# Moving the rates' exponentials to GpSimd, the first state squares to ScalarE, and the fourth token group to the end of the first step

## The chip, the cores and the metric

The kernel runs as one program on one core of a Trainium2 chip. The metric is the device time of one execution in microseconds. The core's engines work from queues of their own and wait for each other by semaphores: TensorE (PE in the profile; PEld is its weight loads), VectorE (DVE), ScalarE (ACT), GpSimd (POOL) and SyncE (SP), which issues the DMAs.

## What is computed

A small two-layer network. Layer 0 is a block with a test-time-trained linear memory and a feed-forward part; layer 1 has attention and experts. The change touches only the memory of layer 0. Cut to what matters:

```python
h = _layernorm(x, axis=-1) * (1 + ca) + sa            # 4 x 512 tokens of 256
qkv = silu(h @ W_qkv); q, k = q / norm(q), k / norm(k)
lr = jax.nn.softplus(h @ W_lr + b_lr + BASE_LR_INV)   # 6 rates a token
w0n = norm(w0); w1n = norm(w1); w2n = norm(w2)        # of the first state
def step(w0, w1, w2, chunk):                          # 8 chunks of 64 tokens
    gate = k @ w0; hb = k @ w2; hidden = silu(gate) * hb
    ...                                               # gradients dhbm, dgba
    w1 += newtonschulz5(einsum(hidden * lr1, v))
    w0 += newtonschulz5(einsum(k * lr0, dgba))
    w2 += newtonschulz5(einsum(k * lr2, dhbm))
    w0, w1, w2 = (w / norm(w) * its first norm for each)
    return w0, w1, w2, silu(q @ w0) * (q @ w2) @ w1
```

The softplus of z is computed as max(z, 0) + log(1 + e), with e = exp(min(-z, z)), and the logarithm as a polynomial in e / (e + 2).

## The kernel before

Sixteen tiles of 128 tokens (a tile holds a chunk of 64 tokens of two sequences) are normed in four groups g = 0 to 3 of four tiles (`StartNorm`). For each group VectorE takes the sums, GpSimd the root of the variance (a power of -1/2 over four columns), an engine normalises the tiles (`normalize`, 256 columns each), TensorE turns the two halves of the result (`turn`, kt = 0 and 1), ScalarE scales and shifts the first half (`modulate`) and VectorE the second (`modulate_half`), into `hT`. Group 0 and 1 hold chunks 0 to 3, groups 2 and 3 chunks 4 to 7.

The rates (`LearningRates`) come in two parts: part 0 is the first four tiles (24 columns), made in the prologue, part 1 the other twelve (72 columns). For each part: TensorE projects, VectorE forms z and u = min(-z, z) (`start`), ScalarE takes v = exp(u) (`exponential`), VectorE u = 1 / (v + 2) (`ratio`), and then the polynomial follows (`finish`), on VectorE for part 0 and on GpSimd, in step 1, for part 1. Each result is told by the semaphore `step`, counted up to OPS = 14 a part.

The recurrence is written out as one `step(t)` for each engine: step 0 (`first`), a hardware loop, and the last two steps written apart. On each engine instructions run strictly in the order written. Inside a step two tables of tuples set the order: `INNER` that of TensorE's products (A, AA, Y, A1, AA1, YT, X2 are phases of the Newton-Schulz iteration, each over six matrices) with other work put between them, and `TAKEN` that of ScalarE's copies out of the PSUM banks. The entries START 0 to 6 exist in step 0 alone: 0 turns modulation rows, 1 and 2 turn group 2, 3 and 4 turn group 3, 5 projects the other rates (`project_rest`, 12 products), 6 turns their result. START 1, 3 and 5 in `TAKEN` are ScalarE's modulations and its copy of the rates. PROJECT_V is the value projection of the chunk after next (two parts before the state's update, two behind it); its first part waits for `h_copied`, GpSimd's copy of that chunk's rows of `hT` (`copy_h`). TURN_QK turns q and k of the next chunk and waits for GpSimd's scaling of them (`scale_qk`).

GpSimd's order in a step is: `hidden`, in step 1 the polynomial of the rates, in step 0 group 2's root and tiles, then `scale_qk`, `apply_rates` (products of k and v with the rates), `copy_h`. Behind steps 0 and 1 stand five operations on modulation rows (`guard_gates`).

The end of a step on VectorE: six updates of the state, sums of squares of three matrices (ScalarE squares others), `factors`, and the scaling. The norms of the first state (`start_sums`, six sums of 128 columns; `start_norms`) are made in step 0. A second set of modulation rows (`make_rows(1)`) is made by TensorE at the end of step 0, copied by ScalarE (`take_rows(1)`), and before both stands a wait for the first operation of the rates' part 1. ScalarE loads a table when a function of another set follows (`load_table`).

## Time and profile before

| | us |
|---|---|
| three runs, median | 1005.22 |
| lowest and highest of them | 1001.09, 1006.02 |
| the profiled execution, its own time | 1001.45 |
| its span, first to last instruction | 999.6 |
| busy in the span: TensorE, VectorE | 958.0, 690.0 |
| busy in the span: ScalarE, GpSimd | 573.2, 465.4 |

Times in the trace count from the span's start. The prologue of the memory lasts to about 24 us, step 0 to about 75, step 1 to about 113, and a later step takes about 38 us. An engine's row shows start and length; a bracket behind it gives the engine's idle time before and what ended it. Two rows of an engine overlap a little, since the next instruction starts while the last drains. L numbers are lines of the kernel before; a helper's line serves many places.

### The profile page before, as it was taken

The page shows a single profiled execution, that of the slowest core. Times are in us where ns is not written, and L with a number is a line of the kernel's source. Part 1 is how long each engine was busy: PE and PEld are TensorE (multiplying, and loading weights), DVE is VectorE, ACT ScalarE, POOL GpSimd, SP SyncE. Part 2 cuts the span into 40 slices and gives each one's busy share as a digit, 9 for nine tenths or more (in the row PEclk, how much of TensorE's full clock was granted, in tenths as well). Part 3 has the DMA queues.
Part 4 walks back from the last instruction along what each step waited for, and adds up shares of the span by engine and source line. Part 5 has one row for each costly group of instructions (what it writes and reads, how often), then busy time and mean ns, then how long its engine had stood idle before and what let it go on. Part 6 is the DMA issues. An engine that isn't in the chain of part 4 may idle for free.

```text
span 999.6 us, 24780 instructions
## 1 busy us (share of the span) xinstructions
PE 958.0 (96%) x9554; PEld 722.3 (72%) x9554; DVE 690.0 (69%) x2061; ACT 573.2 (57%) x1534; POOL 465.4 (47%) x425
## 2 busy tenths in 40 slices
PE   9799999999999999999999899999999999999987
PEld 7668788788787656574647678786878696868646
DVE  5998898998999822314132776867686668676874
ACT  4677888888888732213132575656565655655541
POOL 1837134033354601001103675866677667779720
PEclk9999999999999999999999999999999999999999
DMA  9221100000000005600004231322232213211202
GB/s 312 80 81 80 43 0 0 0 0 0 1 2 2 2 1 144 245 1 1 0 1 97 51 64 45 75 54 57 49 71 61 54 45 74 64 34 44 96 2 86
DMA packets 32811, 52.94 MB, mean 53 GB/s; under 512 B 7760, under 2 KB 17744, under 8 KB 31824
## 3 DMA queue, kind: packets, MB, share of 16 engines
q1 hardware_dynamic: 32720, 51.69, 18.7%
q8 instruction: 61, 1.00, 0.4%
q14 instruction: 30, 0.25, 0.1%
HBM read 22.57 MB, written 2.10 MB: 25 GB/s over the span
## 4 chain that ended last, share of the span: by engine, by line
PE 47%; DVE 7%; ACT 3%; issue 2%; POOL 1%; DMA 1%; SPq 0%; DVEq 0%; POOLq 0%
PE quad L2218 9%; PE quad L2177 8%; PE quad L1807 8%; PE quad L2121 6%; PE quad L2237 5%; PE quad L2251 4%; DVE act_probs L2576 2%; ACT act_probs L2474 1%; PE quad L2315 1%; DVE wq_wo L2591 1%; DVE x_pairs L2608 1%; PE quad L2185 1%; PE quad L1694 1%; PE quad L2140 1%; ACT hT L1707 1%
## 5 line engine op out<-in xcount | busy, mean ns | idle before, releaser
L2830 POOL TENSOR_TENSOR act_probs<-act_probs,rden 128x512 f32<-128x512 f32 (+3 forms) x128 | 170.2, 1336 | 105.4 <-DVE rden L2596 105.4
L2474 ACT ACTIVATE act_probs<-act_probs,neg_max 128x256 f32<-128x256 f32 (+3 forms) x256 | 141.1, 553 | 84.0 <-DVE neg_max L2576 83.6
L2177 PEld LDWEIGHTS quad<-hT,ug_queries 128*128 128x128 f32 x1024 | 122.6, 192 | 14.3 <-issue 7.7
L2177 PE MATMUL quad<-hT,ug_queries 128*128 128x128 f32 x1024 | 124.7, 275 | 1.1 <-DVE act_probs L1822 0.5
L1807 PE MATMUL quad<-hT,ug_raw_switch 128*128 128x512 f32 x256 | 113.9, 595 | 0.0
L1822 DVE SCALAR_TENSOR_TENSOR act_probs<-quad,ws_up,silu_keys 128x512 f32<-128x512 f32 x32 | 24.0, 750 | 98.2 <-ACT silu_keys L1817 98.2
L1817 ACT ACTIVATE silu_keys<-quad,ws_gate 128x512 f32<-128x512 f32 x32 | 22.0, 687 | 118.6 <-PE quad L1807 118.6
L1807 PEld LDWEIGHTS quad<-hT,ug_raw_switch 128*128 128x128 f32 x256 | 47.5, 190 | 55.0 <-issue 54.8
L2218 PE MATMUL quad<-down_raw_out,ug_raw_switch 128*128 128x256 f32 (+3 forms) x256 | 79.6, 439 | 4.6 <-DVE neg_max L2576 4.6
L2218 PE MATMUL quad<-silu_keys,ug_raw_switch 128*128 128x256 f32 (+3 forms) x256 | 79.5, 439 | 4.0 <-DVE neg_max L2576 2.6
L2596 DVE RECIPROCAL rden<-den 128x2 f32<-128x2 f32 x128 | 20.3, 158 | 87.4 <-ACT act_probs L2474 87.3
L2591 DVE STREAM_TRANSPOSE wq_wo<-act_probs 128x1024 f32<-128x1024 f32 (+1 forms) x64 | 70.7, 1106 | 1.6 <-POOL act_probs L2830 1.3
L2576 DVE CUSTOM_DVE_ANT_0 act_probs<-quad,mask 128x128 f32<-128x128 f32 (+3 forms) x160 | 65.3, 445 | 0.0
L2251 PE MATMUL quad<-down_keys,act_probs 128*128 128x256 f32 x256 | 60.5, 380 | 0.9 <-ACT act_probs L2484 0.8
L2218 PEld LDWEIGHTS quad<-down_raw_out,ug_raw_switch 128*128 128x128 f32 x256 | 42.4, 190 | 24.2 <-issue 14.1
L2218 PEld LDWEIGHTS quad<-silu_keys,ug_raw_switch 128*128 128x128 f32 x256 | 42.1, 190 | 24.3 <-issue 13.3
L2121 PE MATMUL quad<-down_raw_out,act_probs 128*128 128x256 f32 x256 | 56.2, 379 | 2.0 <-PEq L1613 2.0
L1489 POOL TENSOR_TENSOR hidden<-gate_silu,hb 128x256 f32<-128x256 f32 x16 | 12.0, 756 | 97.7 <-ACT hb L1034 97.7
L2251 PEld LDWEIGHTS quad<-down_keys,act_probs 128*128 128x128 f32 x256 | 47.9, 190 | 12.3 <-issue 2.9
L2121 PEld LDWEIGHTS quad<-down_raw_out,act_probs 128*128 128x128 f32 x256 | 48.3, 190 | 9.6 <-issue 3.3
L1290 DVE SCALAR_TENSOR_TENSOR q_bf<-quad,silu_keys 128x512 bf16<-128x512 f32 x72 | 46.6, 683 | 8.1 <-PE quad L699 7.8
L2810 POOL TENSOR_TENSOR x_rows<-x_rows,x_pairs 128x512 f32<-128x512 f32 x8 | 10.1, 1267 | 85.3 <-DVE x_pairs L2567 85.3
(352 smaller groups left out, 2378.2 us busy)
## 6 DMA issues: line engine op xcount, KB each, us to landing
rope_swapped<-gate SPq DMA_DIRECT2D x120, 64.0 KB, 2.0
ug_raw_switch<-gate SPq DMA_DIRECT2D x60, 128.0 KB, 2.4
ug_raw_switch<-in_wmod SPq DMA_DIRECT2D x4, 512.0 KB, 10.6
x_pairs<-in_x SPq DMA_DIRECT2D x4, 512.0 KB, 7.9
x_rows<-x_pairs SPq DMA_DIRECT2D x8, 256.0 KB, 5.0
wq_wo<-in_wq_nopeT SPq DMA_DIRECT2D x1, 2048.0 KB, 8.5
wq_wo<-in_wo SPq DMA_DIRECT2D x1, 2048.0 KB, 13.1
ug_queries<-in_switch_w SPq DMA_DIRECT2D x1, 2048.0 KB, 7.8
```

The costliest lines, as they stand in the source:

```text
L1290: nc.vector.scalar_tensor_tensor(q_bf[:, q, :], bank[q][:], ca_b2, a_bf[:, q, :], ALU.mult, ALU.add).then_inc(taken[q], 1)
L1807: mm = k.nc.tensor.matmul(k.bank[2 * (m % 2) + w][:], self.w_ug[:, w, kt, P * m:P * m + P], k.hT[:, kt, 2 * i:2 * i + 2, 4 * C * u:4 * C * ...
L1822: k.nc.vector.scalar_tensor_tensor(self.act_t[:, m, :], k.bank[2 * (m % 2)][:], k.ws_up[:, m:m + 1], self.silu[:, m % 2, :], ALU.mult, ALU ...
L2121: mm = nc.tensor.matmul(bank[4 + q // 2][:, D * (q % 2):D * (q % 2) + D], act_t[:, m, P * q:P * q + P], w_down[:, ffn.place(m), :], start= ...
L2177: mm = nc.tensor.matmul(out[:, P * i:P * i + P], w[:, kt, HP * half + i, :], in_order(k.hT[:, kt, b, cols], i), start=(kt == 0), stop=(kt ...
L2218: nc.tensor.matmul(score_bank[t % AHEAD][e][:, 0:width(n)], query[:, n % 2, e, p, :], keys[b % 2][:, p // 2, 0:width(n)], start=True, stop ...
L2237: mm = nc.tensor.matmul(out[:, pairs, :], val[rows, b % 2, j, :], src[rows, j, e, pairs, :], start=(j == 0), stop=(d == LAST_OF[i]))
L2251: mm = nc.tensor.matmul(out[:, 0:D], oT[:, p, :], w_vo[:, p, :], start=(p == 0), stop=(p == NP - 1))
L2474: nc.scalar.activation(tile, tile, ACT.Exp, bias=neg_max[:, r, e:e + 1], scale=-1.0, accum_out=den[:, r, e:e + 1])\
L2576: nc.vector.tensor_tensor_reduce(probs[:, t % RING, e, 0:cols].rearrange("p (w c) -> p w c", c=P), score_bank[t % AHEAD][e][:, 0:cols].rea ...
L2591: nc.vector.transpose(turned_of[batches[n][1]][:, :, :, p, :].rearrange("p j e c -> p e j c"), probs[:, t % RING, :, 0:width(n)].rearrange ...
L2830: nc.gpsimd.tensor_tensor(tile, tile, rden[:, t % RING, :].unsqueeze(2).to_broadcast([P, 2, cols]), ALU.mult)\
```

## The change

Rates: both exponentials go from ScalarE to GpSimd, as a power of e (a constant column `euler`), and ScalarE's four table loads for them go. For part 1 also the ratio goes from VectorE to GpSimd: v + 2, its power of -1/2, the square of that. VectorE's `start(0)` stands ahead of the scaling of q and k, `start(1)` behind the sums of squares of the state. The first state's sums of squares go from VectorE to ScalarE, into scratch tiles of others, and ScalarE squares three matrices in step 0 as in the other steps. Group 3 is normalised by GpSimd, between `apply_rates(1)` and `copy_h(2)`, and its turns and what follows stand later in `INNER` and `TAKEN`. TensorE projects the first rates ahead of the first values, and q and k of chunk 1 behind the first gates.

```diff
-    def exponential(self, act, part):
+    def exponential(self, pool, part):
         z, u, v, m, lr = self.columns(part)
-        act.wait_ge(self.step, self.OPS * part + 2)
-        self.k.nc.scalar.activation(v, u, ACT.Exp).then_inc(self.lr_act, 1)
+        pool.wait_ge(self.step, self.OPS * part + 2)
+        self.k.nc.gpsimd.tensor_tensor(v, self.k.euler[:].to_broadcast([P, u.shape[1]]), u, ALU.pow).then_inc(self.lr_act, 1)
+
+    def ratio_by_root(self, pool, part):
+        z, u, v, m, lr = self.columns(part)
+        n = self.OPS * part + 2
+        pool.wait_ge(self.lr_act, part + 1)
+        self.k.nc.gpsimd.tensor_scalar(u, v, 2.0, None, ALU.add).then_inc(self.step, 1)
+        pool.wait_ge(self.step, n + 1)
+        self.k.nc.gpsimd.tensor_tensor(u, u, self.k.neg_half[:, 0:1].to_broadcast([P, u.shape[1]]), ALU.pow).then_inc(self.step, 1)
+        pool.wait_ge(self.step, n + 2)
+        self.k.nc.gpsimd.tensor_tensor(u, u, u, ALU.mult).then_inc(self.step, 1)
...
-    SQUARED, SQUARED_FIRST = (4, 5, 3), (4, 5)
+    SQUARED = (4, 5, 3)
...
                 if first:
+                    project_qk(1, 0)
                     first_norm.turn(pe, 1, 0, bank[NORM_PLACES[0]])
...
-            project_v(0)
             first_norm.wait_halves(pe, 2, 2)
             rates.project_first(pe)
+            project_v(0)
             pe.wait_ge(s["qkv_acted"], 3)
             turn_v(0, 0)
             turn_qk(0, 0, 1)
             turn_qk(0, 1, 3)
-            project_qk(1, 0)
             step(0, first=True)
...
                 if first:
                     mods.take_rows(act, 0)
+                    act.wait_ge(w_in, STATE_IN)
+                    for m in range(3):
+                        for hd in range(H):
+                            op = nc.scalar.activation(n0_sq[H * m + hd], state[:, m, hd, :], ACT.Square,
+                                                      accum_out=n0_rows[:, H * m + hd:H * m + hd + 1])
+                    op.then_inc(n0_step, 1)
                 act.wait_ge(s["g_total"], t + 1)
...
-                if first:
-                    rates.exponential(act, 1)
-                    load_table(ACT.Sqrt)
                 root_state(0)
...
-            load_table(ACT.Exp)
             take_v(0, 0)
             take_qk(0, 0, 1)
-            rates.exponential(act, 0)
             take_qk(0, 1, 3)
-            load_table(ACT.Silu)
...
-                    for m in range(3):
-                        start_sums(m)
...
                     start_norms()
-                    first_norm.normalize(dve, nc.vector, 3)
                     first_norm.modulate_half(dve, 2, bank[6])
...
-                    if first and n == 2:
-                        first_norm.modulate_half(dve, 3, bank[6])
...
                     if first and n == 3:
-                        rates.start(dve, 1)
+                        first_norm.modulate_half(dve, 3, bank[6])
...
                     update(q)
-                    if first and n == 3:
-                        reduce_state(3)
                 for q in (2, 0, 1):
                     reduce_state(q)
+                if first:
+                    rates.start(dve, 1)
                 factors(1)
...
+            rates.start(dve, 0)
             for i in range(PAIRS):
                 norm_first(i)
                 scale_first(i)
-            rates.start(dve, 0)
...
             mods.take_turned(dve, 1)
-            rates.ratio(dve, 1)
...
                 if isinstance(t, int) and t == 1:
+                    rates.exponential(pool, 1)
+                    rates.ratio_by_root(pool, 1)
                     rates.finish(pool, nc.gpsimd, 1, False)
...
                     apply_rates(t + 1)
+                    if first:
+                        first_norm.normalize(pool, nc.gpsimd, 3)
...
+            rates.exponential(pool, 0)
             first_norm.root(pool, 1)
```

In the orders below a row is a line of the kernel, an operation, out<-in and the shape; `x4` is four alike in a row. The first place is GpSimd at the start of step 1: `hidden`, then the other rates (`proj_gated` is their tile). Before:

```order
L1489 TENSOR_TENSOR hidden<-gate_silu,hb 128x256 x2
L422 TENSOR_TENSOR proj_gated<-proj_gated 128x72
L423 TENSOR_TENSOR proj_gated<-proj_gated 128x72
L424 TENSOR_SCALAR proj_gated<-proj_gated 128x72
L428 TENSOR_SCALAR proj_gated<-proj_gated 128x72
```

Of the change:

```order
L1486 TENSOR_TENSOR hidden<-gate_silu,hb 128x256 x2
L391 TENSOR_TENSOR proj_gated<-euler,proj_gated 128x72
L397 TENSOR_SCALAR proj_gated<-proj_gated 128x72
L399 TENSOR_TENSOR proj_gated<-proj_gated,neg_half 128x72
L401 TENSOR_TENSOR proj_gated<-proj_gated 128x72
L433 TENSOR_TENSOR proj_gated<-proj_gated 128x72
L434 TENSOR_TENSOR proj_gated<-proj_gated 128x72
```

Two powers (L391 and L399) and two plain operations stand in front of the polynomial, and with it in front of all that GpSimd does later in the step.

The second place is GpSimd at the end of step 0: the rates' products, the copy of chunk 2's rows (`h_chunk`), and the first of the operations on modulation rows. Before:

```order
L1475 TENSOR_TENSOR v_lr<-qkv,lr 128x256 x2
L1475 TENSOR_TENSOR k_lr<-qkv,lr 128x256 x2
L1450 COPY h_chunk<-hT 128x512
L200 TENSOR_SCALAR norm_xn<-silu_keys 64x512
L202 TENSOR_SCALAR norm_xn<-norm_xn 64x512
```

Of the change (`gate` is group 3's normalised tile here):

```order
L1472 TENSOR_TENSOR v_lr<-qkv,lr 128x256 x2
L1472 TENSOR_TENSOR k_lr<-qkv,lr 128x256 x2
L272 TENSOR_SCALAR gate<-x_pairs,ln0a_mv,ln0a_rstd 128x256 x4
L1447 COPY h_chunk<-hT 128x512
L201 TENSOR_SCALAR norm_xn<-silu_keys 64x512
```

Four tiles of group 3 stand in front of the copy.

The third place is TensorE in step 0 around the value projection of chunk 2 (`w_qkv,h_chunk`). Before (`hT,w_lr` is the rates' projection, `eye,out_silu` the turn of its result):

```order
L368 MATMUL quad<-hT,w_lr 32x512 x6
L699 MATMUL quad<-silu_keys 128x128 x4
L564 MATMUL quad<-w_qkv,h_chunk 128x256
L699 MATMUL quad<-y_bf 128x128 x4
L699 MATMUL quad<-silu_keys 128x128 x4
L699 MATMUL quad<-y_bf 128x128 x4
L564 MATMUL quad<-w_qkv,h_chunk 128x256
L380 MATMUL quad<-eye,out_silu 128x3x32 x4
```

Of the change (`eye,gate` are the turns of group 3):

```order
L575 MATMUL quad<-w_qkv,h_chunk 128x256
L710 MATMUL quad<-y_bf 128x128 x4
L710 MATMUL quad<-silu_keys 128x128 x4
L710 MATMUL quad<-y_bf 128x128 x4
L575 MATMUL quad<-w_qkv,h_chunk 128x256
L278 MATMUL quad<-eye,gate 128x128 x4
L710 MATMUL quad<-silu_keys 128x128 x4
L703 MATMUL quad<-eye_bf,y_bf 128x128 x4
L710 MATMUL quad<-y_bf 128x128 x4
L710 MATMUL quad<-silu_keys 128x128 x4
L278 MATMUL quad<-eye,gate 128x128 x4
```

Both turns of group 3, which stood ahead of the projection, are behind it, and the rates' projection is no longer ahead of it but further back, behind the third product of the last phase.

## Rows read from the trace of the kernel before

**Rows 1.** The page: busy us of each engine, share of the span, instructions
```profile
PE 958.0 (96%) x9554; PEld 722.3 (72%) x9554; DVE 690.0 (69%) x2061; ACT 573.2 (57%) x1534; POOL 465.4 (47%) x425
```

**Rows 2.** Windows: stretch, length, busy us (instructions) PE, PEld, DVE, ACT, POOL, clock, DMA
```profile
41.00:57.20 16.20, 13.46 (x174) 11.00 (x171) 15.37 (x36) 9.78 (x22) 15.68 (x17) 1.00 0.01 3
...
57.20:66.70 9.50, 9.48 (x119) 7.98 (x119) 8.22 (x22) 7.74 (x25) 2.18 (x3) 1.00 0.24 83
```

**Rows 3.** GpSimd groups by shape: count, busy us, mean ns, idle before
```profile
L1679 POOL TENSOR_TENSOR norm_rstd<-norm_var,neg_half 128x4 f32<-128x4 f32 x11 | 11.2, 1018 | 46.0 <-DVE norm_var L1674 46.0
```

**Rows 4.** GpSimd timeline, other widths: start us, us, engine, line, operation
```profile
943.29 0.71 POOL L1679 TENSOR_TENSOR norm_rstd<-norm_var,neg_half 128x2 f32<-128x2 f32 x1
...
950.54 0.56 POOL L1679 TENSOR_TENSOR norm_rstd<-norm_var,neg_half 128x1 f32<-128x1 f32 x1
...
968.90 1.47 POOL L1679 TENSOR_TENSOR norm_rstd<-norm_var,neg_half 128x1 f32<-128x1 f32 x1 [17.80 <-DVE norm_var L1674]
```

**Rows 5.** Timeline of step 1, GpSimd, first and last of the rates
```profile
78.97 0.34 POOL L422 TENSOR_TENSOR proj_gated<-proj_gated 128x72 f32<-128x72 f32 x1
...
86.96 0.38 POOL L436 TENSOR_TENSOR lr<-proj_gated 128x72 f32<-128x72 f32 x1
```

**Rows 6.** Timeline of the prologue, GpSimd and VectorE
```profile
18.74 1.01 POOL L1552 TENSOR_TENSOR n_qk<-ss_qk,half 128x4 f32<-128x4 f32 x1 [0.61 <-DVE ss_qk L1182]
...
21.12 1.38 DVE L271 TENSOR_SCALAR act_probs<-x_pairs,ln0a_mv,ln0a_rstd 128x256 f32<-128x256 f32 x4
...
25.13 0.42 DVE L1240 TENSOR_TENSOR d_hb<-quad,gate_silu 128x256 f32<-128x256 f32 x1
```

**Rows 7.** Timeline of step 0: VectorE's lost work, its half, ScalarE's idle time
```profile
30.98 0.27 DVE L1268 CUSTOM_DVE_ANT_0 act_probs<-state 128x128 f32<-128x128 f32 x1
...
32.26 0.08 DVE L1268 DVE_READ_ACCUMULATOR2_ANT start_sums<- 128x1 f32 x1
...
40.54 0.19 ACT L1060 ACTIVATE g_norm<-quad 128x24 bf16<-128x24 f32 x1 [2.38 <-PE quad L772]
...
46.33 2.36 DVE L271 TENSOR_SCALAR gate<-x_pairs,ln0a_mv,ln0a_rstd 128x256 f32<-128x256 f32 x4
...
48.61 0.99 DVE L310 TENSOR_SCALAR hT<-quad,scale1T,modT 128x256 f32<-128x256 f32 x2
```

**Rows 8.** Timeline of step 0, GpSimd
```profile
36.29 5.65 POOL L271 TENSOR_SCALAR gate<-x_pairs,ln0a_mv,ln0a_rstd 128x256 f32<-128x256 f32 x4
...
50.82 0.61 POOL L1450 COPY h_chunk<-hT 128x512 f32<-128x512 f32 x1
```

**Rows 9.** Timeline of the end of step 0: TensorE, VectorE, ScalarE
```profile
55.25 1.92 PE L368 MATMUL quad<-hT,w_lr 128*32 128x512 f32 x12
...
57.33 0.65 PE L564 MATMUL quad<-w_qkv,h_chunk 128*128 128x256 f32 x2
...
65.38 1.28 DVE L1366 SCALAR_TENSOR_TENSOR state<-quad,state 128x512 f32<-128x512 f32 x2
...
67.28 1.28 ACT L390 ACT_TABLE_LOAD   x1
...
68.49 0.62 PE L160 MATMUL quad<-ug_raw_switch,silu_c 128*32 128x512 f32 x2
...
70.48 0.60 ACT L166 ACTIVATE norm_xn<-quad 128x512 f32<-128x512 f32 x1
```

**Rows 10.** Timeline of step 1, GpSimd, scaling and copy
```profile
88.35 2.04 POOL L1463 TENSOR_TENSOR qkv<-qkv,r_qk 128x512 f32<-128x512 f32 x2 [1.01 <-PE quad L699]
...
94.53 0.61 POOL L1450 COPY h_chunk<-hT 128x512 f32<-128x512 f32 x1
```

**Rows 11.** Timeline of step 1, TensorE
```profile
92.63 0.61 PE L579 MATMUL quad<-eye,qkv 128*128 128x128 f32 x4
...
97.02 0.65 PE L564 MATMUL quad<-w_qkv,h_chunk 128*128 128x256 f32 x2
```

**Rows 12.** Windows late in the kernel: PEclk is the share of full clock
```profile
968.00:970.00 2.00, 2.00 (x65) 0.83 (x34) 1.90 (x5) 1.38 (x3) 1.10 (x1) 0.50 0.00 0
```

33 lines of the change are left out of this document (14 added, 19 removed).

## The prediction

> **What bounds the kernel now.** Three views were read, in this order. The page's busy times first: TensorE is busy 96% of the span [rows 1], so time comes and goes where TensorE waits for somebody or is made to do its work in another place. All edits lie in the first 114 us (prologue, first step, second step of the eight), so the timeline of that stretch was read next, engine by engine, with busy times by stretch. From the first products of step 0 to its first value projection (41.0 to 57.2 us) VectorE is busy 15.4 and GpSimd 15.7 of 16.2 us, TensorE 13.5 [rows 2]: two engines have no air there. In the rest of the step TensorE has none (9.48 of 9.50 us). Last, GpSimd's power operation by size, since the change puts three such operations on wide tiles.
>
> All times below are those of the profile before; a shift is added to them.
>
> **What one power costs.** The change computes exponentials and a reciprocal as powers on GpSimd, over 24 columns once and over 72 columns twice. The trace has no power of such a width. It has eleven over four columns, mean 1018 ns [rows 3], one over two columns, 0.71 us, and one over one column, 0.56 us [rows 4]. From one to two columns 0.15 us are added, from two to four 0.31 us: a line of 0.41 us plus 0.15 us a column. (The other one-column power, 1.47 us, ran beside a 1024-column product of VectorE and is left out.) A plain 72-column product takes 0.34 us [rows 5], so nearly all of the slope is the power itself. On that line 24 columns cost 0.41 + 24 x 0.15 = 4.0 us and 72 columns 11.2 us. The ends: no slope beyond four columns (1.0 us for either), or the steeper piece of the line (4.1 and 11.5 us). I take the line, because its two pieces agree; it is an extrapolation by a factor of 18.
> The Trainium skill (GPSIMD Engine Reference, section 3.1) prices a two-input elementwise operation at about 2.6 cycles per element at 1.2 GHz, some 0.16 us for 72 columns beyond the dispatch. It was measured on additions; the four-column row disagrees with it by a factor of about seventy per column. By the page the sum would be that of rival B.
>
> **Part 1, prologue (+2.55 us up to the gradients' norms).** GpSimd finishes the second square root at 19.75 us [rows 6]. Now the 24-column power stands behind it (until 23.8), and the layer norm's root, 1.0 us, behind that (until 24.9). The rates' first two operations are moved ahead of the q/k scaling on VectorE, so their input is ready in time; that move costs nothing there, because the next thing VectorE can do waits for GpSimd. VectorE's normalisation of group 1 then starts at 24.95 in place of 21.12, and what follows it, the rates' polynomial and backward (before at 25.13) [rows 6], is one chain of VectorE's: +3.83 us, backward starts at 28.96. TensorE's part is covered: the projection moved behind the gates, and the two table loads that ScalarE loses (about 1.5 us each), would let the gates start a little earlier, but the gates' results then lie waiting for VectorE. Behind backward, the six sums of state squares leave VectorE: from 30.98 to 32.26 us, six at 0.213, 1.28 us [rows 7]. VectorE is busy without a gap there, so they come back in full: 3.83 - 1.28 = +2.55. On ScalarE the six squares cost about 1.75 us in front of the root that waits for the gradients' sum; there ScalarE sat idle 2.38 us [rows 7], so they are hidden, with some 0.6 us to spare. If that cover were gone, up to 1.8 us.
>
> **Part 2, first step to its value projection (-0.1 us).** VectorE loses the normalisation of group 3 (2.36 us) [rows 7], which would bring that stretch forward. But GpSimd gets it, behind the rates' products and ahead of the copy of the next chunk's rows. Its four tiles of group 2 took 5.65 us [rows 8], so I take the same. The copy, before at 50.82 [rows 8], moves to 56.5 and ends at 57.1. TensorE's projection of chunk 2, before at 57.33 [rows 9], waits for it, so it starts at 57.2. What VectorE gains goes into this wait. If GpSimd were faster with VectorE off its back (4.5 us), about 1 us could come back.
>
> **Part 3, from there to the second step (+4.0 us).** Before, both turns of group 3 and the rates' projection (1.92 us) were done by 57.2 [rows 9]. Now TensorE does them behind the projection, as two places of the order show. The path: projection and the products up to the first turn's end, 57.2 to 59.4; ScalarE is free for it behind its copies at 60.95, and takes 1.0 us as VectorE's half does (0.99) [rows 7]: 62.0; second turn, 62.65; VectorE's half, 63.7; two polynomials of 0.65, 65.0; six state updates of 0.64 (1.28 for two [rows 9]), 68.8, the last one 0.9 us later behind the rates' projection, 69.75. Before, the last update ended at 66.66: +3.1. Then three reductions (2.55 us) and the rates' first two operations (0.45), now in front of the factors: 72.75. TensorE's second set of modulation rows waits for the first of the two, 72.5 in place of 68.49, and ScalarE's copy of them, before at 70.48, everything behind it, and the second step move by +4.0 [rows 9]. The two table loads that ScalarE loses here (one at 67.28 [rows 9]) lie in front of that copy, which waits for TensorE already: nothing. The fourth reduction leaves VectorE (0.9) and is inside the count. Bounds: 0 if the new waits all fall into air, +5 if the turns also hold back the transposes of y.
> On table loads the Trainium skill (ScalarE: Activation LUTs, What ACT_TABLE_LOAD costs) counts about 2.66 us a switch with a drain of 1.38. The row shows 1.28 us, and ScalarE's next operation starts at 68.58, 0.02 us behind it. By the page the removals would be worth more; in the sum they are worth nothing by either.
>
> **Part 4, second step (+20.8 us, and 1.0 for the clock).** GpSimd computes the other 72 rates here, from 78.97 to 87.34 us [rows 5], then waits 1.0 us for TensorE and scales the next q and k at 88.35 [rows 10]. New in front: two powers of 72 columns (22.4), an addition (0.42), a product (0.34), five gaps of 0.08: 23.6 us. The polynomial ends at 110.95, scaling starts at 111.0: +22.6. VectorE loses addition and reciprocal (0.8 us), which lay beside ScalarE's and TensorE's work. Who waits: TensorE's turn of q and k at 92.63 [rows 11] needs the first scaling, done at 89.4, a slack of 3.2 us; its projection of chunk 3 at 97.02 [rows 11] needs the row copy, done at 95.14 [rows 10], a slack of 1.9 us. The second decides: 22.6 - 1.9 = +20.8. No later step takes it back, since each step reads the state of the one before. After the stop TensorE finds its clock low: late in the kernel, after thin work, it was granted 0.50 (1.2 of 2.4 GHz) for a stretch [rows 12]; that costs about 1.0 us here, between 0 and 2.
>
> **Sum.** 2.55 - 0.1 + 4.0 + 20.8 + 1.0 = +28.2 us. On the profiled execution's 1001.45 us that gives 1029.7. The three runs lie from 1001.09 to 1006.02, their median 3.8 us above the profiled one, by which it would be 1033.4; I forecast the middle, 1032.
>
> **The rivals.**
> B, a power is priced like any operation, a fixed 1.0 us and plain speed per column. For it: the plain rows, and a loop may be poor on short rows only. The page of the Trainium skill named above gives this result too. Against it: the straight line through three sizes. Then 24 columns cost 1.06: the prologue gives 3.83 - 2.94 - 1.28 = -0.4; parts 2 and 3 stay, +3.9; in the second step 2 x 1.15 + 1.1 = 3.4, less 1.0 of idle and 1.9 of slack, +0.5. Sum +4.0: 1005.4, or 1009.2 by the median.
> C, the slope halves on wide rows: 24 columns 2.2, 72 columns 5.6. Prologue 3.83 - 1.8 - 1.28 = +0.8, parts 2 and 3 +3.9, second step 20.8 - 11.2 = +9.6, clock 0.5: +14.8, 1016 to 1020.
> D, faster: VectorE bounds the first step and the powers are almost free. Its lost work comes back, 1.28 + 2.36 + 0.9 + 0.45, and one table load of 1.48 at the end: about -6, 995 to 999. It decides only if the 24-column power stays under 1.3 us and the 72-column ones under 0.8, and if the row copy isn't late. VectorE's full stretch [rows 2] speaks for it, the four-column power of 1.02 us [rows 3] and GpSimd's equally full stretch against it.
> That the change would not do what it says is excluded by the order, which shows the three wide powers.
>
> **How the numbers follow.** The forecast case, 1024 to 1041, has 0.68 (slope within 10%, part 3 from 1 to 5 us, the runs' own spread). C has 0.12, B 0.12, D 0.05, and 0.03 goes to powers dearer than the line. The range that should hold eight of ten takes the forecast case and most of C: 1013 to 1041. A measurement of this kernel can tell about 0.5% (5 us) from no change. Faster by more than that: D, 0.05. Within it: most of B, 0.10. Slower: 0.85.
>
> **What would show each step.** GpSimd rows of 4.0 us (24 columns) and 11.2 us (72 columns, twice). Backward starting near 29 us. The six squares on ScalarE ahead of the norm's root without delaying it. The first projection of the chunk rows waiting for GpSimd's copy near 60. The second step's gates about 6.5 us late. In the second step one TensorE gap of some 18 us that GpSimd's scaling ends, a second of one or two us that its copy ends, and a granted clock of 0.5 behind them. A 72-column power near 1 us proves the forecast wrong at its root; a gap of TensorE elsewhere, ended by ScalarE or VectorE, would show that part 3 was mis-sized.

## The result and the profile of the changed kernel

The changed kernel takes 1030.3 us (median of 4 runs, 1029.4 to 1030.6) against 1005.0 us for the kernel before (median of 4, 1001.1 to 1006.0): the recorded ratio is 1.0268, 95% interval 1.0238 to 1.0298 (the quotient of the two medians is 1.0252). It is slower by 2.5 to 2.7%. The profiled execution took 1030.6 us, its span is 1028.8 (before: 1001.45 and 999.6). Between the profiles the change costs 29.2 us, between the medians 25.3: the profiled execution of before is one of its fastest.

Five places of the trace answer the prediction's steps.

The page first (busy us of each engine, share of the span, instructions; then the granted clock in 40 slices of 25.7 us):
```profile
PE 961.8 (93%) x9554; PEld 725.4 (71%) x9554; DVE 686.2 (67%) x2035; ACT 569.9 (55%) x1545; POOL 498.2 (48%) x435
...
PEclk9999699999999999999999999999999999999999
```
TensorE does the same 9554 matmuls in 961.8 us of busy time instead of 958.0 [rows 1], and its share falls from 96% to 93%: the time is in gaps. Only one slice, the fifth (102.9 to 128.6 us), shows a low clock.

GpSimd's powers by width (count, busy us, mean ns, idle time before):
```profile
L391 POOL TENSOR_TENSOR proj_gated<-euler,proj_gated 128x72 f32<-128x72 f32 x1 | 11.9, 11880 | 0.0
...
L399 POOL TENSOR_TENSOR proj_gated<-proj_gated,neg_half 128x72 f32<-128x72 f32 x1 | 11.9, 11867 | 0.1
...
L1682 POOL TENSOR_TENSOR norm_rstd<-norm_var,neg_half 128x4 f32<-128x4 f32 x11 | 11.2, 1016 | 46.1 <-DVE norm_var L1677 46.1
...
L391 POOL TENSOR_TENSOR proj_gated<-euler,proj_gated 128x24 f32<-128x24 f32 x1 | 4.6, 4566 | 0.0
```
The 72-column powers took 11.88 and 11.87 us (predicted 11.2), the 24-column one 4.57 (predicted 4.0), the four-column ones what they took before [rows 3].

The prologue (start us, us, engine, line, operation, idle time before and who ended it), against [rows 6]:
```profile
19.96 4.57 POOL L391 TENSOR_TENSOR proj_gated<-euler,proj_gated 128x24 f32<-128x24 f32 x1
...
25.53 1.38 DVE L272 TENSOR_SCALAR act_probs<-x_pairs,ln0a_mv,ln0a_rstd 128x256 f32<-128x256 f32 x4 [3.97 <-POOL ln0a_rstd L263]
...
29.55 0.42 DVE L1251 TENSOR_TENSOR d_hb<-quad,gate_silu 128x256 f32<-128x256 f32 x1
```
VectorE waits 3.97 us for the layer norm's root behind the power; backward starts at 29.55 instead of 25.13.

The rest of step 0: GpSimd's normalisation of the fourth group, its copy of chunk 2, TensorE's projection behind it, the second turn of that group, the modulation rows, and ScalarE's copy of them, against [rows 8, 9]:
```profile
53.83 4.84 POOL L272 TENSOR_SCALAR gate<-x_pairs,ln0a_mv,ln0a_rstd 128x256 f32<-128x256 f32 x4
...
58.61 0.61 POOL L1447 COPY h_chunk<-hT 128x512 f32<-128x512 f32 x1
...
59.37 0.67 PE L575 MATMUL quad<-w_qkv,h_chunk 128*128 128x256 f32 x2 [1.34 <-POOL h_chunk L1447]
...
64.17 0.66 PE L278 MATMUL quad<-eye,gate 128*128 128x128 f32 x4 [1.64 <-ACT hT L305]
...
75.14 0.62 PE L161 MATMUL quad<-ug_raw_switch,silu_c 128*32 128x512 f32 x2
...
77.14 0.60 ACT L167 ACTIVATE norm_xn<-quad 128x512 f32<-128x512 f32 x1 [1.95 <-PE quad L161]
```

Step 1, against [rows 10, 11]: GpSimd's scaling, its move of the queries (qT) and its copy of chunk 3; ScalarE's first copy of turned queries; TensorE's two turns of q and k and its first projection of chunk 3:
```profile
117.96 2.04 POOL L1460 TENSOR_TENSOR qkv<-qkv,r_qk 128x512 f32<-128x512 f32 x2
...
120.72 0.61 POOL L1455 COPY qT<-qT_next 128x512 f32<-128x512 f32 x1
...
124.13 0.61 POOL L1447 COPY h_chunk<-hT 128x512 f32<-128x512 f32 x1
...
121.43 0.38 ACT L975 ACTIVATE qT_next<-quad 128x256 f32<-128x256 f32 x1 [22.01 <-POOL qT L1455]
...
119.05 1.12 PE L590 MATMUL quad<-eye,qkv 128*128 128x128 f32 x4 [19.60 <-POOL qkv L1460]
...
122.21 0.81 PE L590 MATMUL quad<-eye,qkv 128*128 128x128 f32 x4 [0.34 <-ACT kT L976]
...
125.32 0.65 PE L575 MATMUL quad<-w_qkv,h_chunk 128*128 128x256 f32 x2
```
The rows that stood at the second and the sixth of these places before:
```profile
91.12 0.61 POOL L1458 COPY qT<-qT_next 128x512 f32<-128x512 f32 x1
...
94.06 0.65 PE L579 MATMUL quad<-eye,qkv 128*128 128x128 f32 x4
```
The scaling is 29.61 us later than 88.35, TensorE stands still for 19.60 us, and the projection is 28.30 us later than 97.02. So 28.3 of the 29.2 us between the spans are there before step 2.

For comparing kernels one landmark per step does: VectorE's copy of the sums of the squared gradients ("row copy" below, the row `g_rows<-quad`). Before it starts at 39.88, 85.36 and 123.65 us in steps 0, 1 and 2. The input does not arrive at the same moment in every execution, so each kernel's first projection of queries and keys (13.38 before) is taken off; what is left, against the kernel before:

| kernel | first projection | row copies of steps 0, 1, 2 | later than before, input taken off | span |
|---|---|---|---|---|
| before | 13.38 | 39.88, 85.36, 123.65 | | 999.6 |
| changed | 13.63 | 43.01, 92.01, 151.94 | 2.9, 6.4, 28.0 | 1028.8 |
| before, powers of the second part alone | 13.62 | 40.11, 86.21, 146.01 | 0.0, 0.6, 22.1 | 1021.6 |
| changed, those powers undone | 13.44 | 42.84, 91.86, 130.18 | 2.9, 6.4, 6.5 | 1009.0 |
| changed, first power undone | 14.73 | 41.50, 90.49, 150.49 | 0.3, 3.8, 25.5 | 1027.4 |
| changed, late turn undone | 13.55 | 42.94, 89.04, 150.24 | 2.9, 3.5, 26.4 | 1026.9 |
| changed, all three powers undone | 13.36 | 40.14, 89.17, 127.46 | 0.3, 3.8, 3.8 | 1004.3 |
| before, squares on ScalarE alone | 13.29 | 38.50, 85.14, 123.45 | -1.3, -0.1, -0.1 | 999.9 |
| before, once more | 13.53 | 40.01, 86.64, 124.96 | 0.0, 1.1, 1.2 | 1000.5 |
| before, two trial powers | 13.64 | 40.11, 85.58, 123.90 | 0.0, 0.0, 0.0 | 1000.3 |
| changed, TensorE kept at work in the stop | 13.57 | 42.95, 92.22, 151.96 | 2.9, 6.7, 28.1 | 1028.7 |
| the same, move of the queries first | 13.33 | 42.70, 93.50, 153.03 | 2.9, 8.2, 29.4 | 1029.2 |
| changed, the same work in other places | 13.71 | 43.09, 95.60, 151.06 | 2.9, 9.9, 27.1 | 1027.4 |

### The profile page after: what moved, and what is told of

It is laid out like the page before. It is cut to its first block, busy times and chain, and to the rows that moved or that the text cites. A ratio compares the mean times of both kernels' runs of the same rounds, so it can differ in the third digit from the quotient of the medians.

```text
span 1028.8 us, 24768 instructions
## 1 busy us (share of the span) xinstructions
PE 961.8 (93%) x9554; PEld 725.4 (71%) x9554; DVE 686.2 (67%) x2035; ACT 569.9 (55%) x1545; POOL 498.2 (48%) x435
## 4 chain that ended last, share of the span: by engine, by line
PE 46%; DVE 7%; ACT 3%; issue 2%; POOL 1%; DMA 1%; SPq 0%; DVEq 0%; POOLq 0%
PE quad L2221 9%; PE quad L2180 8%; PE quad L1810 8%; PE quad L2124 5%; PE quad L2240 5%; PE quad L2254 4%; DVE act_probs L2579 1%; ACT act_probs L2477 1%; PE quad L2318 1%; DVE wq_wo L2594 1%; DVE x_pairs L2611 1%; PE quad L2188 1%; PE quad L1697 1%; PE quad L2143 1%; DMA rope_swapped<-gate 1%
## 5 line engine op out<-in xcount | busy, mean ns | idle before, releaser
L1810 PEld LDWEIGHTS quad<-hT,ug_raw_switch 128*128 128x128 f32 x256 | 47.5, 190 | 55.0 <-issue 54.8
```

The source lines that it names most:

```text
L1810: mm = k.nc.tensor.matmul(k.bank[2 * (m % 2) + w][:], self.w_ug[:, w, kt, P * m:P * m + P], k.hT[:, kt, 2 * i:2 * i + 2, 4 * C * u:4 * C * ...
```

## The experiments

**The powers of the second part alone.** The kernel before with this edit, and ScalarE's exponential of that part and VectorE's ratio taken out:
```diff
                 if isinstance(t, int) and t == 1:
+                    rates.exponential_by_power(pool, 1)
+                    rates.ratio_by_root(pool, 1)
                     rates.finish(pool, nc.gpsimd, 1, False)
```


> The kernel before with one part of the change alone: the rates' second part (72 columns) takes its exponential and its ratio by two powers on GpSimd in step 1, and ScalarE's exponential and VectorE's reciprocal of that part go. Prologue, squares and end of step 0 as before. Theory (the powers stand on the path to the scaling that TensorE waits for): two rows of 11.9 us for 128x72, the scaling in step 1 some 23 us later than 88.35, the value projection of step 1 some 21.6 us later, one gap of TensorE of 19 to 20 us ended by the scaling, span 999.6 + 21.5 = 1021 us. Rival 1 (a large share of the 29 us comes from the other parts and only shows behind them): under +15, span below 1015. Rival 2 (the copy behind the powers decides, as the prediction had it): a second gap of 1 to 2 us ended by GpSimd's copy.


Measured: 1025.9 us (4 runs, 1023.4 to 1028.7), ratio 1.0214 (1.0181 to 1.0247), span 1021.6, as the theory had it. From the row copy of step 1 to that of step 2 it is 59.80 us instead of 38.29: these powers cost 21.5 us by themselves. TensorE's list of waits (us in total, times, longest) has one large entry and no wait for the copy in that step:
```profile
PE quad L595 <- POOL qkv L1475: 19.6, 1, 19.6
```
Rival 1 falls, and so does the second gap that the prediction and rival 2 expected. The 0.6 us in step 1 has its own cause, below.

**Those powers undone in the changed kernel.**
```diff
             root_state(0)
             if first:
+                rates.exponential_act(act, 1)
                 mods.take_rows(act, 1)
...
-                    rates.exponential(pool, 1)
-                    rates.ratio_by_root(pool, 1)
...
             mods.take_turned(dve, 1)
+            rates.ratio(dve, 1)
```


> The changed kernel with the rates' second part given back to ScalarE (exponential, in its idle time of 1.95 us before the row that ends it at 77.14) and VectorE (reciprocal); everything else as changed. Theory: the stop in step 1 goes whole, span 1028.8 - 21.6 = 1007.2 us, against before +7.6 (prologue, end of step 0 and a last 1 us stay). Rival (the late end of step 0 and the powers hide each other in part, so that each undone alone gives back less than it costs alone): 1010 or more. By the prediction's own numbers 20.8 + 1.0 would come back: 1007.0.


Measured: 1010.8 us (5 runs), ratio 1.0059 (1.0028 to 1.0090), span 1009.0. Up to step 2 it is the theory: 6.5 us late instead of 28.0. The span gives back some 2 us less than that (from the row copy of step 2 to the end it is 878.8 us here and 876.9 in the changed kernel). The clock shows where: TensorE was granted 0.52 from 392 to 394 us and 0.62 to 396, a stretch of the stages that no kernel here changes, where the changed kernel's profile has 1.00.

**The first part's exponential undone.**
```diff
+            load_table(ACT.Exp)
             take_v(0, 0)
             take_qk(0, 0, 1)
+            rates.exponential_act(act, 0)
             take_qk(0, 1, 3)
+            load_table(ACT.Silu)
...
-            rates.exponential(pool, 0)
```


> The changed kernel with the first part's exponential (24 columns) given back to ScalarE; the early start of that part on VectorE, the squares on ScalarE and all else as changed. Theory: the normalisation of the second token group no longer waits 3.97 us for GpSimd, the backward pass of step 0 starts near 25.1 less nothing from the squares, which came after it, so the row copy that stood at 39.88 before and at 43.01 after comes near 38.6 (1.28 of state sums less). The projection of chunk 2 then waits for GpSimd's copy behind its third normalisation, so not all of the 4.4 us comes back at the end: 3 to 4.4, span 1024.4 to 1025.8. Rival (VectorE in step 0 has slack elsewhere, the prologue was hidden): span within 1 us of 1028.8.


Measured: 1030.0 us (4 runs, 1029.2 to 1030.9), ratio 1.0249 (1.0227 to 1.0271), span 1027.4 with the input 1.1 us later. With that taken off, the row copies of all three steps come 2.5 to 2.6 us earlier: less than the theory's 3 to 4.4, more than the rival's nothing. Why it isn't 4.4: ScalarE's exponential stands later than it did before the change, because the changed kernel lets TensorE project the rates ahead of the values, so the values' activation ends at 22.61, and VectorE waits for it:
```profile
22.63 1.28 ACT L1027 ACT_TABLE_LOAD   x1
...
25.04 0.23 ACT L391 ACTIVATE proj_gated<-proj_gated 128x24 f32<-128x24 f32 x1
...
25.30 0.18 DVE L425 TENSOR_SCALAR proj_gated<-proj_gated 128x24 f32<-128x24 f32 x1 [1.37 <-ACT proj_gated L391]
...
28.02 0.43 DVE L1259 TENSOR_TENSOR d_hb<-quad,gate_silu 128x256 f32<-128x256 f32 x1
```
Backward starts at 28.02, which is 26.92 on the changed kernel's time of input, 2.63 us ahead of its 29.55: just what the row copies show. TensorE waits longer for GpSimd's copy of chunk 2:
```profile
57.86 0.67 PE L580 MATMUL quad<-w_qkv,h_chunk 128*128 128x256 f32 x2 [2.45 <-POOL h_chunk L1455]
```
It is 1.34 in the changed kernel. The difference costs nothing: the projection, too, is 2.6 us earlier with the input taken off. It is TensorE that comes sooner, since in this execution its clock stayed at 1.00 in step 0, and in the changed kernel's it was at 0.50 from 44.0 to 47.5 us (see the kernel before, once more).

**The late turn undone.** The changed kernel with the two tables of the order (INNER, TAKEN) as before, and
```diff
                 if first:
                     start_norms()
+                    first_norm.normalize(dve, nc.vector, 3)
                     first_norm.modulate_half(dve, 2, bank[6])
...
-                    if first:
-                        first_norm.normalize(pool, nc.gpsimd, 3)
...
-                if first:
-                    rates.start(dve, 1)
                 factors(1)
```
with the second half's modulation and the rates' start back among VectorE's polynomials.


> The changed kernel with the fourth token group normalised on VectorE again and turned where it was before, in the middle of step 0, and the start of the rates' second part back among VectorE's polynomials. Theory (turning the group near the end of the first step makes rates, modulation rows and the new state's turn late): 4.6 us come back, plus what the projection of chunk 2 gains when GpSimd's copy is early again, less up to 2.4 us of normalisation that VectorE takes up: span 1023.5 to 1025.5. Rival (the row of operations behind the state update sets the end of the step anyway, and the order only moved the waits): within 1 us of 1028.8.


Measured: 1027.9 us (4 runs), ratio 1.0224 (1.0200 to 1.0249), span 1026.9, which is 1.9 below the changed kernel and not 3 to 5. Step 1 gets the gain (row copy 2.97 us earlier, 2.89 with the input taken off), step 2 little more than half of it (1.70). What was lost stands behind the stop. Windows of the changed kernel (stretch, length, busy us of PE, PEld, DVE, ACT, POOL, granted clock, DMA):
```profile
118.00:122.00 4.00, 2.82 (x20) 2.50 (x20) 0.78 (x2) 0.57 (x2) 3.83 (x6) 0.50 0.00 0
...
122.00:126.00 4.00, 3.79 (x54) 3.64 (x55) 2.88 (x5) 2.50 (x7) 3.91 (x6) 0.93 0.01 4
```
and of this one, which resumes at 116.11 instead of 119.05:
```profile
115.00:119.00 4.00, 2.82 (x20) 2.49 (x20) 0.72 (x2) 0.51 (x2) 3.81 (x6) 0.50 0.00 0
...
119.00:123.00 4.00, 3.72 (x37) 3.67 (x38) 1.65 (x3) 2.08 (x6) 3.91 (x6) 0.60 0.01 2
```
By half microseconds, the clock was at 0.50 from 102.5 to 122.5 in the one and from 102.0 to 122.0 in the other: 3.4 us of the work behind the stop fell into it in the one, 6 us in the other.

**All three powers undone.** Both edits together (first and second part).


> The changed kernel with all three wide powers given back (24 columns to ScalarE, 72 to ScalarE and VectorE's reciprocal): what is left of the change are the squares on ScalarE, the fourth group normalised by GpSimd and turned near the end of step 0, and the early start of the rates' first part. Theory (the parts add up; row copies less those of before, corrected for when the input arrives: 2.9 in step 0, 6.4 in step 1 and 28.0 in step 2 of the changed kernel; less 2.6 for the first power and 21.6 for the two others): +0.3, +3.8, +3.8 us, span near 1003.5. Rival (the late turn costs only because the prologue had already made step 0 late, or the two hide each other): +2 or less in step 1.


Measured: 1007.6 us (5 runs), ratio 1.0043 (1.0028 to 1.0058), span 1004.3, row copies +0.3, +3.8, +3.8. The parts add up to a tenth of a microsecond, and the rival falls. What stays is the late turn, the squares on ScalarE and the new order of the prologue, and it is slower than before without any power, by 0.3 to 0.6%.

**The cost line of a power.** The kernel before with
```diff
             pool.wait_ge(mods.step, 5)
+            for x, n in zip(trial, (8, 36)):
+                nc.gpsimd.tensor_tensor(x[:], k.half[:, 0:1].to_broadcast([P, n]), k.neg_half[:, 0:1].to_broadcast([P, n]), ALU.pow)
```


> The kernel before with two powers more, on GpSimd, in its idle time between step 0 and step 1 (59 to 77 us): 128x8 and 128x36, of constants, into tiles that nobody reads. It measures the cost line of a power. Line through the four known widths of the traces before and after (1: 0.56, 4: 1.02, 24: 4.57, 72: 11.88): 0.15 us a column and about 0.4 to 0.9 us fixed. Theory 1 (the fixed part is about 0.9, and the narrow rows of 1 to 4 columns lie under the line): 128x36 takes 6.4 us, 128x8 2.1 us. Theory 2 (fixed 0.41, as the prediction had it, and the wide rows of the change cost more for their broadcast operand): 128x36 takes 5.8 us, 128x8 1.6. The time of the kernel stays that of before within its scatter, since nothing waits for them.


Measured (count, shortest/median/longest ns, starts, forms):
```profile
L1560 POOL TENSOR_TENSOR trial<-half,neg_half x2: 1661/3884/6106, 59.7 to 61.3; 128x8 f32<-128x8 f32 x1, 128x36 f32<-128x36 f32 x1
```
So 8 columns take 1.66 us and 36 take 6.11. The one run took 1002.1 us, within the scatter of before. Through 1, 2, 4, 8, 36 and 72 columns (0.56, 0.71, 1.02, 1.66, 6.11, 11.87) runs one line, 0.39 us plus 0.16 us a column, with no more than 0.05 us of error. Theory 2 has the fixed part right, and its slope was 0.01 too small; its dearer broadcast operand isn't seen, as the rows with one (8 columns and more) and those without lie on one line. A few rows lie above it: the 24-column power by 0.3 us, in the changed kernel and in each that keeps it (4.57), a four-column one of the kernel with the first power undone (1.42 instead of 1.02), a 72-column one in a run below (12.31). Each of these stands beside VectorE's products of 128x512; no run tests whether that is the cause.

**TensorE kept at work during the stop.** The changed kernel, step 1 of TensorE written out, and in front of its turn of q and k
```diff
+                        if isinstance(t, int) and t == 1 and n == 0:
+                            for _ in range(WARM):
+                                nc.tensor.matmul(bank[7][:], k.ones[:], w_qkv[:, 0, 0:2 * D], start=True, stop=True)
                         turn_qk(t + 1, n, 7)
```


> The changed kernel with step 1 of TensorE written out instead of being the first turn of its loop, and with 22 matmuls of 128x512 into a bank that is free then, in front of the turn of queries and keys that waits for GpSimd's scaling. They fill some 17 of the 19.6 us of the stop (a 128x256 of this type takes 0.38 us), so that the clock is not low when the work resumes. Theory: the first granted clock after the scaling is 1.0, the turn and products behind it run at their usual pace, and the value projection of chunk 3, 6.27 us behind the resumption in the changed kernel, is ready after 4.4 us, but then waits about 0.7 to 1.3 us for GpSimd's copy: the low clock had hidden the prediction's second gap. Row copy of step 2 at 151.94 - 0.6 to 1.2 = 150.7 to 151.3. Rival (the low clock itself cost the whole 1.9 us and the copy is no limit): 150.0. Rival 2 (the code of the written-out step costs a fetch of its own): 152 or later.


Measured: 1030.5 us (4 runs), ratio 1.0261 (1.0235 to 1.0287), span 1028.7, mean clock 0.998 instead of 0.988, row copy of step 2 at 151.96 instead of 151.94. Nothing comes back. GpSimd's move of the queries and TensorE's second turn:
```profile
120.97 0.61 POOL L1460 COPY qT<-qT_next 128x512 f32<-128x512 f32 x1
...
122.39 0.66 PE L591 MATMUL quad<-eye,qkv 128*128 128x128 f32 x4 [1.54 <-ACT kT L981]
```
The turn waits 1.54 us for ScalarE's copy, which waits for that move. In the changed kernel the same wait is 0.34 us, because the slow clock had stretched the first turn and the products over it. Taken from the start of the scaling, the row copy of step 2 comes after 33.98 us in the changed kernel and 33.75 here: half clock behind the stop cost 0.2 us. Two more kernels fit in: 33.83 with the powers alone, where 2.8 us of the work behind the stop fell into the low clock, and 34.05 with the first power undone (3.5 us). My theory named the right kind of limit and the wrong operation: not the copy of chunk 3 but the move before it.
The Trainium skill (TensorE: Matmul & The Clock Gate, Terms) takes the penalty as the throttled time times the missing share of the clock. By that an estimate for the 20 us at 0.50 is 10 us; these runs show 0.2, since nearly all of that time lay in the stop.

**The move of the queries first.** The same, with the move in front of the first of the rates' rows in that step:
```diff
+                if isinstance(c, int) and c == 2:
+                    move_q()
                 rate_rows(c, kl0, 2, 0)
```


> The kernel with 22 filling matmuls in the stop of step 1, and in that step GpSimd's move of the queries directly behind the scaling, in front of the first of the rates' rows instead of behind it. That kernel showed: with the clock at 1.0 behind the stop the row copy of step 2 stays at 151.96, as in the changed kernel (151.94), and TensorE's second turn of keys and queries waits 1.54 us for ScalarE's copy, which waits for GpSimd's move (120.97 to 121.58). Theory (the move decides how much of the 23 us reaches TensorE, not GpSimd's copy of chunk 3): the move ends 0.55 to 0.6 us earlier, the second turn starts near 121.8 instead of 122.39, and everything behind it, the row copy of step 2 too, comes 0.5 to 0.6 us earlier: 151.4. Rival (another limit stands right behind the move: the copy of chunk 3, done at 125.0, or VectorE's operations): the row copy of step 2 comes less than 0.2 us earlier.


Measured: 1031.0 us (1 run), span 1029.2. This execution lost 1.8 us in step 0 (row copy of step 1 at 93.50). Its clock was at 0.50 from 58.5 to 62.0 us, behind the wait for the copy of chunk 2 and not ahead of it, and the work from there to the second turn of group 3 was stretched:
```profile
59.05 1.19 PE L576 MATMUL quad<-w_qkv,h_chunk 128*128 128x256 f32 x2 [2.44 <-POOL h_chunk L1452]
```
In the changed kernel the same two products take 0.67 us. So only the distance from the scaling counts: 153.03 - 119.45 = 33.58 us against 33.75. The move, directly behind the scaling, let TensorE's second turn start 2.51 us behind the first instead of 3.09 (123.06 and 120.55; 122.39 and 119.30), but only 0.17 of these 0.58 us arrived, for then the next limit came:
```profile
126.39 0.67 PE L576 MATMUL quad<-w_qkv,h_chunk 128*128 128x256 f32 x2 [0.21 <-POOL h_chunk L1452]
```
GpSimd's copy of chunk 3, the limit that the prediction had named, stands 0.2 us behind the move: at 0.17 us the rival holds, and the theory is right only in that the move was the first limit.

**The same work in other places.** The changed kernel with the exponential between the steps and the rest behind the copy of chunk 3, the rates' columns in another tile, and a wait for the rates' rows in front of the guard:
```diff
-        rates = LearningRates(k, scope, spare=add[:].rearrange("p i d -> p (i d)")[:, D // 2:], rows=h_o)
+        rates = LearningRates(k, scope, spare=k.gates[2][:].rearrange("p b d -> p (b d)")[:, 0:4 * NT * 3 * H], rows=h_o)
...
             first_norm.wait_halves(pool, 5, 5)
+            rates.exponential(pool, 1)
             step(1)
             pool.wait_ge(s["h_copied"], 2)
+            pool.wait_ge(s["lr_applied"], 3 * PAIRS * 3)
...
+                    if isinstance(t, int) and t == 1:
+                        move_q()
+                        copy_h(t + 2)
+                        rates.ratio_by_root(pool, 1)
+                        rates.finish(pool, nc.gpsimd, 1, False)
                     apply_rates(t + 1)
```


> The changed kernel with the same three parts of the work on GpSimd for the rates' second part, the two powers of 128x72 among them, in other places: the exponential between step 0 and step 1 (from 75.1, where its input is ready and GpSimd is idle), and the addition, the second power, the squaring and the series in step 1 behind the scaling, the move of the queries and the copy of chunk 3, in front of the rates' rows that need them. The rates' working columns move to a tile that is free longer. No work is taken away. Theory (the 24 us cost time only because they stand in front of the scaling that TensorE waits for): no stop of 19.6 us, hidden product of step 1 at 87 instead of 84.1 (0 to 2 us of wait for it), scaling near 95, rates' rows done near 122, in time for the gradients of step 2 near 124.6; row copy of step 2 at 130 to 132, span 1007 to 1009.5. Rival (24 us more on GpSimd in these two steps don't fit beside its other work, and the stop only moves to step 2): row copy of step 2 at 136 or later.


Measured: 1027.7 us (4 runs), ratio 1.0236 (1.0210 to 1.0262), span 1027.4. The theory is wrong and the rival right: the row copy of step 2 stands at 151.06, where 130 to 132 was expected, and the stop moved. Step 1 was late already, its row copy 3.5 us behind the changed kernel's. About half of that is a clock of 0.50 from 59.5 to 63.0 us, behind the wait for the copy of chunk 2; the rest comes from the exponential, whose input was ready only at 77.1, so that GpSimd's hidden product stood behind it until 89.86 (84.07 in the changed kernel):
```profile
77.58 12.31 POOL L391 TENSOR_TENSOR gate<-euler,gate 128x72 f32<-128x72 f32 x1 [10.23 <-DVE gate L415]
```
The scaling started at 98.60, 7.16 us of GpSimd's idle time ahead of it, and GpSimd's rows of the rates ended near 128. The waits of all engines from 118 to 137 us, and from 76 to 155 (us in total, times, longest):
```profile
ACT qkv L958 <- POOL k_lr L1472: 5.5, 1, 5.5
...
PE quad L606 <- ACT weight L1013: 5.0, 1, 5.0
...
POOL hidden L1486 <- DMA gate<-norm_xn: 8.2, 1, 8.2
...
PE quad L678 <- POOL hidden L1486: 7.9, 3, 6.6
```
ScalarE opens each step with the activation of the next queries and keys, which overwrites what GpSimd's rate rows still read; TensorE's gates wait 5.0 us behind it. GpSimd's guard of the second layer's gates, and the transfers that wait for it, slid behind the powers too, and the next product of GpSimd waited 8.2 us for them. I had looked for who reads the rates, not for who overwrites their inputs.

**The squares alone, a version faster than both.** The kernel before with ScalarE's six squares in place of VectorE's:
```diff
                 if first:
                     mods.take_rows(act, 0)
+                    act.wait_ge(w_in, STATE_IN)
+                    for m in range(3):
+                        for hd in range(H):
+                            op = nc.scalar.activation(n0_sq[H * m + hd], state[:, m, hd, :], ACT.Square, accum_out=n0_rows[:, H * m + hd:H * m + hd + 1])
+                    op.then_inc(n0_step, 1)
...
-                    for m in range(3):
-                        start_sums(m)
```


> The kernel before with one part of the change alone: the six squares of the first state that feed its norms are taken by ScalarE (in front of its square root of the gradients' norms) and leave VectorE; no power is added and nothing else moves. Theory (the 1.28 us that leave VectorE stand on the path of step 0, and ScalarE has the time): the row copy of step 0 comes 1.3 us earlier than 39.88, the one of step 1 0.6 to 1.3 us earlier than 85.36, span 998.3 to 999.0. Rival (VectorE's 1.28 us are absorbed, because another engine sets the end of step 0): the row copy of step 1 within 0.3 us of before. Either way the medians stand within 0.3% of each other.


Measured: 1001.1 us (12 runs, 998.8 to 1003.3) against 1003.2 (17 runs, 1000.5 to 1007.6), ratio 0.9975 (0.9961 to 0.9990). It is faster, by a quarter of a per cent. The profile at first looks like the rival: 1.3 us earlier in step 0, nothing left in step 1. The next run explains it.

**The kernel before, once more.**


> The kernel before, unchanged, for another profiled execution and more times: its runs so far spread from 999.5 to 1007.6 us, those of the changed kernel from 1029.3 to 1030.9 only. Theory 1 (the spread arises behind the changed stages, in the layers that both kernels share): the row copies of steps 0 to 2 at 39.9, 85.4, 123.7 again, and the difference to the other profile in the later part. Theory 2 (it arises in the first 80 us, which the change reorders): the row copies of steps 1 and 2 differ by the difference of the spans.


Measured: 1004.8 us (10 runs, 1001.4 to 1005.9), span 1000.5. The row copy of step 0 is the same, that of step 1 is 1.13 us later with the input taken off, and stays so to the end. Windows of this execution, in the columns above:
```profile
40.00:42.00 2.00, 1.77 (x15) 1.77 (x16) 1.89 (x14) 1.09 (x5) 2.00 (x2) 0.57 0.00 0
...
42.00:44.00 2.00, 2.00 (x21) 1.94 (x19) 1.35 (x5) 1.84 (x4) 2.00 (x3) 0.58 0.00 0
```
and in the first:
```profile
42.00:44.00 2.00, 2.00 (x34) 1.91 (x32) 1.97 (x8) 2.00 (x5) 2.00 (x2) 1.00 0.00 0
```
That is the cause. In step 0 TensorE waits some 1.6 us for the row copy, and in some executions its clock is at 0.50 for about 3.4 us around and behind that wait, in others not. It was in this one, in the squares' (38.5 to 42.5), in that of the powers alone (41.0 to 44.5), in the changed kernel's (44.0 to 47.5), and in those with the second part's powers undone, the late turn undone and TensorE kept at work; it was not in the first of before, in that with the trial powers, and in those with the first power or all three undone. From the row copy of step 0 to that of step 1 it is 45.48 and 45.47 us in the two executions of before's order without it, and 46.63, 46.64 (squares) and 46.10 (powers alone) in the three with it. Where the projection waits for the late copy of chunk 2 it costs next to nothing: 48.99 and 49.03 us without, 49.00, 49.02 and 49.27 with it. Against an execution that had it too, the squares are 1.26 us ahead in step 1 (85.14 and 86.64, less 0.24 of input): their 1.28 us come back in full. This dip explains 1.1 us of the spread of the kernel before, so theory 2 holds for that much; the slower of the runs of before, up to 8 us over the fastest (999.5 to 1007.6 us), have no profile, and where they lose the rest is open.

## Why the prediction was right

It said 1032 with 1013 to 1041, and slower with 0.85; measured are 1030.3 and slower. Its sum on the profiled execution was 1029.7, and the profiled execution of the changed kernel took 1030.6. The adjustment towards the median of the runs, +2.3, was not needed: the changed kernel's runs lie within 1.2 us of each other, where those of before spread over 5. So the sum of 28.2 us fits the 29.2 between the profiles better than the 25.3 between the medians. The dip of the clock in step 0, which costs the kernel before 1.1 us and the changed kernel next to nothing, can be a part of the other 3.9; the rest is open, and that the forecast hit the median within 2 us is in part luck.

- **The price of a power** decided everything and was right in kind: a straight line in the columns. Its fixed part was right (0.41 for 0.39), its slope 0.15 instead of 0.16, so a wide power was 0.67 us short. Rivals B (1 us), C (5.6) and D (under 0.8) are excluded by the rows of 11.9. By the Trainium skill's price of a two-input elementwise operation (GPSIMD Engine Reference, section 3.1) an estimate for 72 columns is 0.16 us; that is what a power costs here for one column.
- **Part 1** was +2.55; the trace shows 3.13 less 0.25 of input, +2.9. Backward was to start at 28.96 and started at 29.55 (29.30 without the input's delay), by the longer power. Undoing that power brought 2.6 of it back. The squares: six on ScalarE from 41.20 to 43.06, then 0.62 us of idle time in front of the root, as the prediction's "some 0.6 us to spare"; their 1.28 us on VectorE are shown by the squares alone.
- **Part 2** was -0.1 and is -1.1 (projection 2.04 us late behind a row copy 3.13 late). The term that was off most is the normalisation on GpSimd, 4.84 us for four tiles and not 5.65; the prediction had named this case, with "about 1 us". The wait for the copy is there (1.34 us, at 59.37).
- **Part 3** was +4.0 and is +4.6 (6.66 less 2.04). The path is the predicted one: ScalarE's half from 63.09, second turn 64.17, six updates, reductions, the rates' start, then the rows at 75.14. Short was the stretch of updates: 66.97 to 72.40, 5.4 us, where 3.84 of work and 0.9 of waiting for the rates' projection were counted; VectorE waited 1.47 us for TensorE there, in three pieces. Parts 2 and 3 together are +3.5; undoing the late turn brought 2.9 of them back in step 1, and the other 0.6 also stands in the kernel with the powers alone, which has no late turn but the dip of the clock in step 0. The two kernels with the late turn and without the dip show 3.5 as well.
- **Part 4** was +20.8 and 1.0 for the clock, and is +21.6 (28.30 less 6.66). The scaling moved by 22.95 (predicted 22.6); that holds 24.78 us of new operations, where 23.6 were counted, and a polynomial of 7.47 us, where the 8.37 of before were taken. TensorE's gap was 19.60 us and not "some 18"; the prediction's own 22.6 less its slack of 3.2 gives 19.4. The right sum came, by luck, from two steps that were wrong and made up for each other. The slack was taken at the copy of chunk 3 (1.9 us); the limit that came first was the move of the queries, ahead of it in GpSimd's queue: from scaling to second turn it is 5.71 us before and 4.25 after, 1.46 of slack. And the low clock cost 0.2 us, not 1.0, as TensorE would have waited for that move anyway. The "second gap of one or two us that its copy ends" did not appear for the same reason; it appeared, ended by ScalarE's copy behind the move, when the clock was kept up. That the clock would be 0.5 behind the stop was right.
- After step 2 the spans differ by another 0.9 us. One of TensorE's waits tells of it: in a stretch of the later layers it waited for VectorE's maxima 1.5 us once before, and 2.5 us in two waits after. I don't count it to the change: from the row copy of step 2 to the end it is 875.5 to 876.5 us in the five executions built on before, and 876.1 to 876.9 in seven of the eight built on the changed kernel (the eighth is the 878.8 above). Whether some half microsecond of it does come from the change is open.

Summed by the trace: 0.25 (input) + 2.9 - 1.1 + 4.6 + 21.6 + 0.9 = 29.2 us.

## What to carry to other kernels

A transcendental power on GpSimd costs by the column (here 0.16 us for each column of 128 rows): 1.0 us for four columns, 11.9 for 72, where ScalarE's exponential of 72 columns took 0.26 us and its table load 1.28. Three rows at different small widths in a trace were enough to see it before the change was made. When an engine's queue is delayed, look at every operation in it that releases somebody, in the order of the queue: the first one whose slack runs out sets the cost, and a later one of smaller slack may never show. An operation that is moved behind others must be checked against who overwrites its inputs as well as against who reads its result.

## What the runs showed of the hardware that I had not expected

- A granted clock of 0.50 that follows a wait of only 1.6 us of TensorE, in some executions of the same kernel and not in others, for some 3.4 us each: 0.6 to 1.2 us later where TensorE is the limit behind it, next to nothing where TensorE waits for GpSimd shortly after (the changed kernel). Where it fell behind that second wait instead, from 58.5 to 62.0 us, the row copy of step 1 came 1.8 us later.
- Behind a stop of 19.6 us the clock came back 20.0 us after it had fallen, in four kernels alike (102.5 to 122.5, 102.0 to 122.0, 101.0 to 121.0, 96.0 to 116.0; the changed kernel, the late turn undone, the first power undone, the powers alone), although TensorE resumed at 119.05, 116.11, 117.53 and 113.28. So the stop cost 1.2 us more in the kernel that resumed earliest within that stretch (from scaling to the row copy of step 2 it is 35.22 us there, 33.98 in the changed kernel).
- A normalisation of four tiles on GpSimd took 5.65 us for group 2 and 4.84 for group 3, with the same instructions, and the same two times within 0.02 us in every execution that has both; why is open.
